# Attention: the next head pair's projection placed inside the current step's dense products, with the output transposes at the head of a step

## The reference

```
x = x + 0.5 * _L0_ffn_ref(_layernorm(x), ...)      # stage F, first run
x = x + _L0_attn_ref(_layernorm(x), ...)           # stage S
x = x + 0.5 * _L0_ffn_ref(_layernorm(x), ...)      # stage F, second run
x = x + 0.5 * _L1_ffn_ref(_layernorm(x), ...)      # stages M, U, M follow

def _layer(x, ...):                                # two of these in each F
    h = shift_token(x)
    q, k, v = jnp.split(h @ wqkv, 3, axis=-1)      # 8 heads of 64
    q, k = l2norm(q) * qs, l2norm(k) * ksc
    q, k = rotary_xpos(q, k)
    x = x + local_attention(q, k, v) @ wo          # windows of 64 keys and the window before
    h = layernorm(shift_token(x))
    a, g = jnp.split(h @ w1 + b1, 2, axis=-1)
    x = x + (a * gelu(g)) @ w2 + b2
```

## Time and profile before

| | |
|---|---|
| runs, device us | 1152.47, 1157.02, 1161.21 (median 1157.02) |
| span of the profiled execution | 1152.9 us |
| busy share of the span | TensorE 86%, its weight loads 55%, VectorE 62%, ScalarE 59%, GpSimd 45% |
| chain that ended last, by engine | TensorE 66%, ScalarE 15%, issue 7%, VectorE 6%, DMA 3%, GpSimd 2% |
| stage F, first run | about 14 to 400 us of the span |
| stage F, second run | about 464 to 800 us |

### The profile page before, as it was taken

One profiled execution on the slowest core, in us unless ns is written; L12 is line 12 of the kernel. 1 busy time (PEld: TensorE's weight loads), 2 busy tenths in 40 slices (PEclk: granted clock), 3 DMA queues, 4 the chain that ended last, 5 costly groups with the idle time before them and its releaser, 6 DMA issues.

```text
span 1152.9 us, 26028 instructions
## 1 busy us (share of the span) xinstructions
PE 995.2 (86%) x9072; PEld 628.5 (55%) x9072; DVE 719.8 (62%) x1657; ACT 681.6 (59%) x1311; POOL 514.8 (45%) x392
## 2 busy tenths in 40 slices
PE   4789999999998877789999999999829986856995
PEld 1445555555555347255555555556418983535995
DVE  1568677778777554477777777778674432665442
ACT  3566686686684572666676676674616654633662
POOL 2455456456442524455553453452463550363552
PEclk9989999999999987899999999999958997776998
DMA  5665454354434600444443443443422222012224
GB/s 177 159 154 135 123 146 112 91 131 112 93 94 99 78 1 3 92 112 112 111 106 86 106 111 85 102 111 75 150 89 61 67 71 74 18 49 63 61 67 128
DMA packets 89711, 109.99 MB, mean 95 GB/s; under 512 B 20368, under 2 KB 74384, under 8 KB 88816
## 3 DMA queue, kind: packets, MB, share of 16 engines
q1 hardware_dynamic: 82160, 91.17, 33.5%
q0 software_dynamic: 4544, 9.35, 2.3%
q10 hardware_dynamic: 2880, 7.81, 2.2%
HBM read 62.66 MB, written 12.07 MB: 65 GB/s over the span
## 4 chain that ended last, share of the span: by engine, by line
PE 66%; ACT 15%; issue 7%; DVE 6%; DMA 3%; POOL 2%; SPq 1%; ACTq 0%; DVEq 0%; POOLq 0%
PE banks L589 7%; PE banks L936 6%; PE banks L946 6%; PE banks L662 5%; PE banks L676 5%; PE banks L620 4%; PE banks L751 3%; PE banks L669 3%; PE banks L637 3%; PE banks L726 2%; PE banks L721 2%; PE banks L645 2%; ACT arena L1184 2%; ACT arena L1189 2%; PE banks L971 1%
## 5 line engine op out<-in xcount | busy, mean ns | idle before, releaser
L2062 POOL TENSOR_TENSOR arena<-arena 128x1024 f32<-128x1024 f32 x64 | 150.9, 2358 | 323.7 <-DVE arena L1662 317.4
L2051 POOL TENSOR_TENSOR arena<-arena 128x1024 f32<-128x1024 f32 x64 | 150.9, 2357 | 40.8 <-ACT arena L1184 40.8
L1654 DVE TENSOR_REDUCE arena<-banks 128x4 f32<-128x512 f32 x128 | 82.4, 685 | 95.1 <-PE banks L620 95.0
L1176 ACT ACTIVATE arena<-banks,arena 128x512 f32<-128x512 f32 x128 | 80.5, 679 | 92.0 <-PE banks L669 91.5
L589 PE MATMUL banks<-arena 128*128 128x512 f32 x256 | 127.2, 621 | 6.7 <-DVE arena L1554 5.9
L2041 POOL DMA_INDIRECT moe_outs<-arena x78 | 81.2, 1040 | 98.2 <-DVE arena L1904 94.1
L1397 ACT ACTIVATE arena<-banks,arena 128x128 f32<-128x128 f32 x312 | 89.0, 369 | 55.8 <-PE banks L936 55.5
L2034 POOL DMA_INDIRECT moe_rows<-arena x64 | 63.9, 998 | 94.6 <-DVE arena L1635 70.3
L1662 DVE TENSOR_TENSOR arena<-arena 128x1024 f32<-128x1024 f32 x64 | 78.0, 1219 | 24.6 <-DMA arena<-arena 24.6
L1189 ACT ACTIVATE arena<-banks 128x1024 f32<-128x1024 f32 x64 | 65.6, 1025 | 44.8 <-PE banks L589 43.9
L946 PE MATMUL banks<-arena 128*128 x624 | 86.7, 282 | 3.5 <-ACT arena L1397 2.9
(11 more groups left out here) (220 smaller groups left out, 1914.5 us busy)
## 6 DMA issues: line engine op xcount, KB each, us to landing
arena<-arena SPq DMA_DIRECT2D x256, 128.0 KB, 3.9
arena<-rstd SPq DMA_DIRECT2D x128, 256.0 KB, 4.2
arena<-moe_rows SPq DMA_DIRECT2D x78, 64.5 KB
arena<-in_mw SPq DMA_DIRECT2D x2, 2048.0 KB, 11.5
arena<-moe_outs SPq DMA_DIRECT2D x16, 256.0 KB, 4.8
arena<-in_rot ACTq DMA_DIRECT2D x12, 256.0 KB, 3.2
arena<-in_wa ACTq DMA_DIRECT2D x2, 1026.0 KB, 6.7
arena<-ssm_a SPq DMA_DIRECT2D x4, 512.0 KB, 6.6
```

The source lines that it names most:

```text
L1654: nc.vector.tensor_reduce(mx[:, e], by_row(bank[3 + e][:]), AX.X, ALU.max).then_inc(s_max, 1)
L2051: nc.gpsimd.tensor_tensor(TA[:, n % 2], RAW, ROTV[:, :, 0, c * C:(c + 1) * C], ALU.mult).then_inc(cos_done, 1)
L2062: nc.gpsimd.tensor_tensor(TA[:, n % 2], TA[:, n % 2], TB, ALU.add).then_inc(rot_sum, 1)
```

## The change

`project` is now called for step `s + 1` inside step `s`: in norm steps (and steps 4 and 5) between the two products of the norm, in hidden steps behind the first of the three hidden pairs, in value steps between the second and third of the four products for V, in output steps between `mlp_output` and `output`, and in the other early steps just ahead of `transpose_scores`. Only `project(0)` stays at a step's head. So a step begins with `transpose_out` and its wait, and the values of both heads follow each other in every step from 3 to 31; in step 32 nothing changes. Only TensorE's program is edited.

```diff
--- before.py
+++ after.py
@@ -574,8 +574,11 @@
                 mm(to[:, 2 * n:3 * n], ones, mine, start=True, stop=True).then_inc(rank_mm, 1)
 
             def ffn(norm0, run):
-                def project(s, n):
-                    hp, c, d = s % HP, s // HP % NCH, s // (HP * NCH)
+                def project(s):
+
+                    if s >= STEPS:
+                        return
+                    n, hp, c, d = STEPS * run + s, s % HP, s // HP % NCH, s // (HP * NCH)
                     if d == 0:
                         need(pe, ln_out, norm0 + c + 1)
                     else:
@@ -583,10 +586,10 @@
                     if run == 0 and s % (HP * NCH) == 0:
                         pe.wait_ge(wa_in[d], 16)
                     after(pe, copied, 2 * n)
-                    src = (YA, YM)[d][:, c * C:(c + 1) * C]
                     for k in range(2):
                         w0 = k * INNER + hp * P
-                        mm(bank[k], w_qkv[d][:, w0:w0 + P], src, start=True, stop=True).then_inc(proj, 1)
+                        mm(bank[k], w_qkv[d][:, w0:w0 + P], (YA, YM)[d][:, c * C:(c + 1) * C],
+                           start=True, stop=True).then_inc(proj, 1)
 
                 def transpose_out(s, n, at, to=7):
                     pe.wait_ge(o_norm, 2 * n + 2)
@@ -646,9 +649,9 @@
                                   start=True, stop=True)
                     last.then_inc(ss_mm, 1)
 
-                def project_v(g, s):
+                def project_v(g, s, t0):
                     d, c, gg = g // NCH, g % NCH, 2 * NCH * run + g
-                    for t in range(TILES):
+                    for t in range(t0, t0 + 2):
                         if t == 0:
                             pe.wait_ge(ss_log, STEPS * run + s + 1)
                         elif t == 1:
@@ -681,10 +684,11 @@
                     pe.wait_ge(yb_ready, gg + 1)
                     pe.wait_ge(ot_evac, STEPS * run + s - 3)
                     mm(bank[7][:], centre, YB[:, c * C:(c + 1) * C], start=True, stop=True).then_inc(mn_cen, 1)
-                    values(s - 3, STEPS * run + s - 3, 1)
                     if s < STEPS:
+                        project(s + 1)
                         pe.wait_ge(ss_log, STEPS * run + s + 1)
                     else:
+                        values(s - 3, STEPS * run + s - 3, 1)
                         bank2_read(pe, run, s)
                     pe.wait_ge(mn_sq, gg + 1)
                     mm(bank[2][:], mean, MSQ, start=True, stop=True).then_inc(mn_var, 1)
@@ -753,9 +757,9 @@
 
                 for s in range(STEPS + 1):
                     n, hp, g = STEPS * run + s, s % HP, s // HP
-                    if s < STEPS:
-                        project(s, n)
-                    elif run:
+                    if s == 0:
+                        project(0)
+                    if s == STEPS and run:
                         pe.wait_ge(copied, 2 * n)
                         pe.wait_ge(sq_done, n)
                         pe.wait_ge(x_ffn, NCH + 1)
@@ -764,11 +768,10 @@
                         first_centred(norm0, 1, run)
                     if s >= 4:
                         transpose_out(s - 4, n - 4, s)
-                    filled = g >= 2 and hp in (1, 3) or hp == 2 and s >= 6
                     if s >= 3:
                         values(s - 3, n - 3, 0)
-                    if filled:
-                        values(s - 3, n - 3, 1)
+                        if s < STEPS:
+                            values(s - 3, n - 3, 1)
                     if s < STEPS:
                         square_sum(s, n)
                     if s == 1:
@@ -780,17 +783,23 @@
                         mlp_norm(g - 2, s)
                     elif s in (4, 5):
                         first_norm(s - 2, s)
-                    elif s >= 3 and not filled:
-                        values(s - 3, n - 3, 1)
                     if hp == 1 and g >= 2:
-                        for j in range(3):
-                            hidden(g - 2, s, j)
+                        hidden(g - 2, s, 0)
+                        project(s + 1)
+                        hidden(g - 2, s, 1)
+                        hidden(g - 2, s, 2)
                     if hp == 2:
-                        project_v(g, s)
+                        project_v(g, s, 0)
+                        project(s + 1)
+                        project_v(g, s, 2)
                     if hp == 3 and g >= 2:
                         mlp_output(g - 2, s)
+                    if hp == 3:
+                        project(s + 1)
                     if hp == 3 and g >= 1:
                         output(g - 1, s)
+                    if hp < 2 and g < 2 and s not in (4, 5):
+                        project(s + 1)
                     if s >= 2:
                         transpose_scores(s - 2, n - 2)
 

```

## The result

The changed kernel takes 1214.8 us (median of four runs: 1213.0, 1213.7, 1216.0 and a disturbed one of 3379.7, which the ratio leaves out), the kernel before 1155.3 in the same series: a ratio of 1.0498, 95% interval [1.0459, 1.0538]. The profiled span is 1211.2 us against 1152.9, 58.3 more.

The account below looks back on a forecast made before the run. The prediction took the stage to go at TensorE's pace, with the projection at a step's head covering other engines' work. Twelve rounds of 3.99 us (48) plus 8 for early steps gave 1157 + 56 = 1213 us, range 1196 to 1230.

Parts of the forecast that it names:

- Norm step: Output transposes at the step's head wait for VectorE's residual reading bank 7; 8.76 us against 8.57, +0.19.
- Hidden step: Output transposes at the step's head wait for VectorE's normalising product reading bank 7; 13.52 us against 12.42, +1.10.
- The Gelu's wait: TensorE's wait for ScalarE's Gelu before the second hidden pair, worth 0.50 us, would be gone.
- Value step: Output transposes wait for VectorE's last gate; waits between V products taken as gone; 10.67 us against 9.69, +0.98.
- Output step: Values wait for the shift of V as before, so the projection behind mlp_output adds its whole 1.72 us.
- Steps 0 to 7: Early steps of each run, chiefly 4, 5 and 7: about 4 us more a run, between 0 and 7.
- Sum: Twelve rounds of 3.99 us give 48, early steps of two runs 8: +56 us in all.
- Filler wins: Rival: bank 7's readers finish in time, only filled gaps count; 1.13 us a round, 14 faster, 1143 us; chance 0.05.
- the four waits: TensorE idle at step heads: residual 0.8, normalising product 1.6, gate 1.2 before output transposes; shift of V 1.7 before values.
- Only the shift of V shows: Rival: bank 7 waits are shorter, leaving 0.6 us a round, 7; with early steps 1164 to 1172 us; chance 0.06.
- The projection waits: Rival: the moved projection waits for the previous copy-out, needed up to 5 us sooner; no cost seen; chance 0.01.
- The clock gives way: Rival: idle fronts drop TensorE's clock to 1.2 GHz, 3.4 us more a round, 41, about 1254 us; chance 0.06.

Follow-up runs that it names:

- the kernel with the added products: Changed kernel plus two unread TensorE products (0.84 us together) at the head of steps 8 to 31 of each run: 1217.1 us, ratio 1.0526.
- its own kernel: Four kernels, each the kernel before with only projections moved into norm, hidden, value or output steps from step 8: ratios 1.0093, 1.0038, 1.0148, 1.0032.
- the added products in the kernel before: Kernel before plus the same two unread TensorE products at the head of steps 8 to 31 of each run: 1194.1 us, ratio 1.0337.
- the second filler: Kernel before with first-head score transposes between the first and second hidden pairs, and in value steps ahead of the fourth V product: 1156.9 us, ratio 1.0003.
- the first: Kernel before with the first head's score transposes between the first and second hidden pairs, projection left in place: 1153.8 us against 1156.6, ratio 0.9968.

## Why the prediction held, point by point

| step | before | forecast | measured |
|---|---|---|---|
| norm | 8.57 | 8.76 | 8.72 |
| hidden | 12.42 | 13.52 | 13.31 |
| value | 9.69 | 10.67 | 10.85 |
| output | 12.17 | 13.89 | 13.89 |
| round | 42.85 | 46.84 | 46.77 |

The steps after are read from T to T, T being the start of the score transposes' row plus 0.875: for the hidden step 640.34 - 627.03 = 13.31.

- *Norm step.* The forecast had the transposes at T + 0.83; they start 0.87 behind it (666.82, with T at 665.08 + 0.875 = 665.955). Right.
- *Hidden step.* 1.60 forecast, 629.54 - 627.905 = 1.63 measured. The Gelu's wait is gone, as forecast. The term is 0.21 too large: the first pair takes 1.82 to the projection (632.98 to 634.80), not 1.98, and from the second pair to T it is 641.215 - 636.51 = 4.70, not 4.82. Both numbers came from rows that began with, or held, products behind an idle time.
- *Value step.* 1.24 forecast, 642.50 - 641.215 = 1.29 measured. The term is 0.18 too small: the gate ends about where it was assumed, but the front lasts 645.93 - 642.50 = 3.43 instead of 3.40, and the dense part and the projection take 652.065 - 645.93 = 6.13 instead of 6.03. The first pair of products takes 1.82 to the projection (645.93 to 647.75), as the first hidden pair does, where 1.72 was counted; the second pair takes 1.72 (649.47 to 651.19), so the waits between the products for V are gone.
- *Output step.* The values start at 654.36, T + 2.30, as forecast, and the whole projection is added.
- *Steps 0 to 7.* About 4 us a run were counted. From step 4's output transposes to step 8's it is 102.3 - 52.9 = 49.4 us in the first run (45.0 before): 4.4 more. In the second it is 573.3 - 528.0 = 45.3 (39.2 before): 6.1 more. The same code in the kernel with the added products, which starts these only at step 8, took 572.6 - 529.4 = 43.2 there, 4.0 more. The other 2.1 of the second run are 0.8 of a longer wait and 1.3 of a lower clock, told below.
- *Sum.* Steps 8 to 32 gave 24.1 and 22.6 us in the two runs, steps 4 to 7 4.4 and 6.1: 57.2 of the span's 58.3. Forecast were 48 and 8.
- *What was luck.* The mechanism is the one forecast, wait by wait. That the sum comes so near is in part luck, for errors cancel. The hidden step's 0.21 too much meets the value step's 0.18 too little. Twelve equal rounds are too many: step 31 has no projection to place, and the last round of the second run lost 45.08 - 42.04 = 3.04 and not 3.92. In return two stretches at the lower clock, which the sum doesn't hold, brought about 1.3 us each.

Of the rivals, *Filler wins* falls with the four waits and with the added products that cost nothing. *Only the shift of V shows* falls with the waits of 0.70, 1.48 and 1.12 for bank 7. Each comes up alone in its own kernel. *The projection waits* doesn't show: no projection within the round has an idle time. *The clock gives way* doesn't happen in the rounds of the second run (1.00 in the window). It does in one round of the first run and in one early step of the second, for about 1.3 us each (below); that rival had 41.

Of the Trainium skill's rules weighed in the prediction, the one on weight loads (Perfetto Trace Analysis, Identifying the Most-Contended Engine; the page names the share of peak FLOPs beside it) would have left room for the added products in the kernel before, by a share of 55%; they cost nearly their whole slot there (38.5 us for 48 steps, 0.80 each), so for this stage the measurement decides against that reading. The rule to rotate groups through PSUM banks so that one bank's evacuation lies beside the next group's matmuls (same page, Optimizing Tensor Performance) agrees with the runs: the transposes that follow on bank 7 at once wait 0.70 to 1.48 us for it.

## What to carry to other kernels

Before a group of work is moved off the head of a stage to fill a gap elsewhere, list what ends behind it on the other engines and asks for what comes next: its slot there may be the only cover they have. The price of the move is the wait that it lays bare less the gap that it fills, step by step, and both can be read from the trace before (here to 0.2 us a step). A short gap is better filled with work whose absence uncovers nothing, and "nothing" has to be read at the next step's head, as the second filler showed, and the first in the first run.

## What the runs showed beside that

In the first steps of each run both kernels show the lower clock, but not at the same instructions. The product of the earlier trace rows that took 1.12 us behind 1.91 us of idle time has this row in the changed kernel:

```profile
505.48 1.60 PE L542 MATMUL banks<-arena 128*128 128x512 f32 x2 [1.82 <-ACT arena L1088]
```

From step 5 of either run on, the kernel before shows 1.00. The changed kernel shows the lower clock there twice, both times behind idle times shorter than the 4.27 us of the earlier trace rows. In the second run's step 5 (TensorE's timeline):

```profile
539.59 0.63 PE L599 MATMUL banks<-arena 128*128 128x128 f32 x4 [2.18 <-DVE arena L1563]
540.15 2.00 PE L640 MATMUL banks<-arena 128*64 128x65 f32 x32
542.08 1.08 PE L648 MATMUL banks<-arena 128*32 128x256 f32 x8
```

The values took 2.00 us instead of 1.15, the square sum 1.08 instead of 0.64; the granted clock from 540 to 544 is 0.57, then 1.00 again. From these transposes to the next dense product it is 544.78 - 539.59 = 5.19 us; at the same place in the kernel with the added products, behind the same 2.18 us of idle time, it is 544.11 - 540.20 = 3.91 at full clock:

```profile
540.20 0.63 PE L599 MATMUL banks<-arena 128*128 128x128 f32 x4 [2.18 <-DVE arena L1567]
540.76 1.15 PE L640 MATMUL banks<-arena 128*64 128x65 f32 x32
```

So it cost 1.3 us here. In the changed kernel TensorE had also stood 1.27 us a little earlier, ahead of step 4's centred product, where the other kernel shows 0.48. Whether that made the difference was not tried.

The second place is the hidden step in the first run's last round; the granted clock from 349 to 352 is 0.50:

```profile
347.18 0.63 PE L599 MATMUL banks<-arena 128*128 128x128 f32 x4 [1.48 <-DVE arena L1732]
348.16 1.36 PE L640 MATMUL banks<-arena 128*64 128x65 f32 x32 [0.34 <-ACT arena L1185]
349.56 1.08 PE L648 MATMUL banks<-arena 128*32 128x256 f32 x8
```

From these transposes to the next dense product it is 352.66 - 347.18 = 5.48 us, in the kernel with the added products, at full clock, 351.01 - 346.84 = 4.17: again 1.3. The wait of 1.48 stands in every round, and in the others the clock stays at 1.00. So the last wait's length alone doesn't tell when the clock falls. Of the other kernels only the one with the values ahead of the transposes shows the lower clock at this place.
